# Row stores from ScalarE's queue, a rearranged first group, and a last group in two halves

## The reference

```python
h = conv1d(x, L0_cond_weight, groups=4, taps=9) + ctx + bias    # ctx = cond_128 @ c_weight.T
logits = h @ W_gate + b_gate                                    # 8 experts, the best 2 for each row of 512
y = relu(einsum(h, W_e) + b_e) of the 2 chosen, averaged
x = x + y
m = einsum('boi,bih->boh', agg_w, x) + agg_b[:, :, None]        # 32x32 kernel of each sample, from an MLP on cond_128
W = scales * q - zeros                                          # int4 weights, 512x512
out = x + (m @ W + bias)
```

## Time and profile before

| | us |
|---|---|
| median of 3 runs | 496.83 (495.22 to 497.33) |
| the profiled execution's own time | 496.38 |
| its span, first to last instruction | 494.6 |
| TensorE busy | 480.0 |
| VectorE busy | 322.6 |
| ScalarE busy | 177.1 |
| GpSimd busy | 197.1 |

### The profile page before, as it was taken

The page is one execution under the profiler, slowest core; times in us unless marked ns, Lnnn a source line. Parts: engine busy times, 40 slices in busy tenths (PEclk is TensorE's granted clock), DMA queues, the critical chain, the costliest instruction groups (busy, mean ns, idle before and its releaser), DMA issues.

```text
span 494.6 us, 10082 instructions
## 1 busy us (share of the span) xinstructions
PE 480.0 (97%) x2341; PEld 324.6 (66%) x2342; DVE 322.6 (65%) x966; ACT 177.1 (36%) x309; POOL 197.1 (40%) x215
## 2 busy tenths in 40 slices
PE   7999999999999999999999999999999969999996
PEld 6999999998854444444444444444446748888885
DVE  5688788888748557563453535454356758888885
ACT  5687888889612112121212212112123212211221
POOL 8055555555537533233233332332233334433430
PEclk8899999999999999999999999999999999999999
DMA  6899988997867775787756657565656599999932
GB/s 165 228 324 306 279 279 281 329 303 252 256 160 223 228 218 130 184 233 188 205 151 167 194 143 202 158 184 168 184 154 197 169 346 326 292 326 312 312 121 97
DMA packets 90050, 110.94 MB, mean 224 GB/s; under 512 B 25198, under 2 KB 61726, under 8 KB 88980
## 3 DMA queue, kind: packets, MB, share of 16 engines
q1 hardware_dynamic: 71520, 68.10, 49.3%
q0 software_dynamic: 11952, 37.28, 21.1%
q10 hardware_dynamic: 6536, 5.09, 3.9%
HBM read 65.44 MB, written 46.51 MB: 226 GB/s over the span
## 4 chain that ended last, share of the span: by engine, by line
PE 83%; DVE 6%; DMA 3%; issue 2%; SPq 2%; ACT 1%; ACTq 1%; DVEq 1%; POOL 0%; POOLq 0%
PE bank L1311 40%; PE bank L1285 15%; PE bank L1272 7%; PE bank L1375 5%; PE bank L1371 5%; PE bank L1354 5%; PE bank L1383 2%; PE bank L1361 2%; DMA out<-orow_list 1%; SPq L454 1%; DMA keys<-lists_d 1%; DMA we<-pairs_d 1%; DVE phases L387 1%; DVE ring_a L1004 1%; DVE lT L990 0%
## 5 line engine op out<-in xcount | busy, mean ns | idle before, releaser
L1311 PE MATMUL bank<-we,lT 128*128 x536 | 232.3, 594 | 0.9 <-DVE ring_a L1004 0.8
L1311 PEld LDWEIGHTS bank<-we,lT 128*128 128x128 f32 x536 | 101.1, 190 | 127.5 <-issue 127.3
L575 POOL DMA_INDIRECT pairs_d<-ring_b,pair_i x71 | 71.8, 1012 | 150.5 <-DVE pair_i L993 106.4
L1004 DVE TENSOR_TENSOR ring_a<-bank,be_bc 128x512 f32<-128x512 f32 x71 | 49.1, 691 | 98.4 <-issue 47.3
L671 ACT ACTIVATE ring_b<-ring_a 128x512 f32<-128x512 f32 x71 | 44.7, 630 | 191.5 <-DVE ring_a L1004 176.3
L556 POOL DMA_INDIRECT lists_d<-token_list,row_i x64 | 69.4, 1085 | 71.4 <-issue 33.4
L1285 PE MATMUL bank<-wconv,phases 128*128 128x128 f32 x768 | 93.9, 280 | 0.8 <-ACT phases L387 0.8
L1285 PEld LDWEIGHTS bank<-wconv,phases 128*128 128x128 f32 x768 | 90.8, 196 | 2.5 <-issue 1.5
L387 DVE COPY phases<-xt 32x512 f32<-32x512 f32 (+1 forms) x96 | 52.6, 547 | 9.2 <-PE bank L1285 5.9
L591 POOL TENSOR_TENSOR we<-xt,we 128x512 f32<-128x512 f32 x26 | 33.4, 1284 | 59.7 <-DVE we L1128 54.3
L387 ACT COPY phases<-xt 32x512 f32<-32x512 f32 x64 | 56.6, 884 | 1.5
(11 more groups left out here) (212 smaller groups left out, 378.5 us busy)
## 6 DMA issues: line engine op xcount, KB each, us to landing
xt<-lists_d SPq DMA_DIRECT2D x268, 64.0 KB
xt<-in_x SPq DMA_DIRECT2D x58, 256.0 KB, 4.9
we<-pairs_d SPq DMA_DIRECT2D x26, 512.0 KB, 5.8
we<-in_L_ffn_W_e SPq DMA_DIRECT2D x8, 1024.0 KB
out<-orow_list SPq DMA_DIRECT2D x32, 256.0 KB, 5.1
words<-pairs_d POOLq DMA_DIRECT2D x6, 512.0 KB, 5.1
lists_d<-orow_list SPq DMA_DIRECT2D x8, 257.0 KB
be_bc<-in_L_ffn_b_e ACTq DMA_DIRECT2D x4, 512.0 KB
```

The lines of the kernel that those rows point to most:

```text
L575: pool.indirect_dma_start(pairs_d, bass.IndirectOffsetOnAxis(ap=pair_i[:, s % DR:s % DR + 1], axis=0), ring_b[:, s % U, :], None, bounds_c ...
L1004: dve.tensor_tensor(ring_a[:, j % 2, :], ps_exp[j % 2][:, :], be_bc[:, bass.ds(expert, 1), :].rearrange("p a n -> p (a n)"), ALU.add).then ...
L1311: mm = pe.matmul(ps_exp[j % 2][:, :], lT[:, j, p * P:(p + 1) * P], we[:, bass.ds(expert, 1), p, :].rearrange("m a n -> m (a n)"), start=(p ...
```

## The change

1. SP issues three of the four loads of convolution weights instead of two; ScalarE issues one, and the load of `bg_bc` moves behind its taps.
2. Phases 3 (ScalarE) and 0 and 1 (DVE) of group 0 are copied ahead of the taps. DVE picks 8 of the 12 taps and ScalarE 4. Phase 2 of group 0 is all DVE's, between its taps and the `wconv` copies, so that `step1` of ScalarE skips group 0.
3. TensorE's first warm-up has 20 transposes instead of 24, and two more follow the filter transposes of each shift.
4. All row stores but the last are issued by ScalarE. SP issues the loads of the last phase without stores between them.
5. GpSimd's add of group a waits for the finished `y` of group a-2 (and of the first six) instead of a-1.
6. The last group's linear product is made in two halves of 256 columns, in two PSUM banks; each half is scaled, added and stored by itself. Its terms go to `ps_mix[0]`, are copied by ScalarE to `last_sum` and added to `y` by GpSimd.

```diff
--- before.py
+++ after.py
@@ -248,6 +248,8 @@
         ps_mix, ps_lin, ps_terms, ps_low = bank[4:6], bank[0:4], bank[6:8], bank[0:2]
+        last_bank = [ps_lin[(NG - 1) % U], ps_lin[NG % U]]
+        last_sum = ring_a[:, 0, :]
@@ -369,10 +376,13 @@
+        taps_of_dve = [range(3), range(3), range(2)]
+        taps_of_act = [range(3, PH), range(3, PH), range(2, PH)]
         def pick_taps(copy, phases_of, taps_ready):
             for t in range(SHIFTS):
-                for p in phases_of:
+                for p in phases_of[t]:
                     k0 = PH * t - p + PH - 1
@@ -394,7 +404,7 @@
             sp.wait_ge(wfull_zero, 1)
-            for s in range(2):
+            for s in range(3):
                 rows = slice(s * CG, (s + 1) * CG)
@@ -469,10 +479,6 @@
-            def store_row(g):
-                sp.wait_ge(out_ready, g + 1)
-                sp.dma_start(out_g[g], orow[:, g % 2, :]).then_inc(out_out[g % 2], 16)
             def load_group(a):
@@ -483,24 +489,19 @@
             sp.wait_ge(exp_done, NT)
-            store_row(0)
             for i, done in enumerate(result_out):
...
             load_pairs(PRIMED + 1)
-            store_row(1)
-            for a in range(PRIMED + 2, PRIMED + DEPTH + 2):
+            for a in range(PRIMED + 2, NG):
                 load_group(a)
-            def row_step(g, j):
-                store_row(g)
-                a = g + PRIMED + DEPTH
-                if a < NG:
-                    load_group(a)
-            unrolled(row_step, 2, NG)
-            for s in out_out:
-                sp.wait_ge(s, 16 * (NG // 2))
+            for half in range(2):
+                cols = slice(half * L // 2, (half + 1) * L // 2)
+                sp.wait_ge(half_out, half + 1)
+                sp.dma_start(out_g[NG - 1][:, cols], orow[:, (NG - 1) % 2, cols]).then_inc(out_out[(NG - 1) % 2], 16)
+            for i, s in enumerate(out_out):
+                sp.wait_ge(s, 16 * (NG // 2 + i))
@@ -586,22 +587,26 @@
                 pool.wait_ge(pairs_in[a % FR], (a - PRIMED) // FR * 16 + 16)
-                pool.wait_ge(y_ready, a)
+                pool.wait_ge(y_ready, max(PRIMED, a - 1))
                 wait(pool, out_ready, a - FR + 1)
                 pool.tensor_tensor(y_of(a), xt[:, x_buffer(a), :], found[:, a % FR, 0, :], ALU.add).then_inc(ya_ready, 1)
+            pool.wait_ge(last_read, 1)
+            pool.tensor_tensor(y_of(NG - 1), y_of(NG - 1), last_sum, ALU.add).then_inc(last_y, 1)
...
             act.wait_ge(wfull_zero, 1)
-            for s in range(2, C // CG):
-                rows = slice(s * CG, (s + 1) * CG)
-                act.dma_start(wfull[rows, rows, PH - 1:PH - 1 + TAPS], conv_w[rows]).then_inc(convw_in, 16)
-            act.dma_start(bg_bc[:, :], b_gate.rearrange("(a e) -> a e", a=1).to_broadcast((P, E))).then_inc(bg_in, 16)
+            rows = slice(3 * CG, 4 * CG)
+            act.dma_start(wfull[rows, rows, PH - 1:PH - 1 + TAPS], conv_w[rows]).then_inc(convw_in, 16)
             act.wait_ge(ident_ready, 2)
             act.copy(g0[:, 0:1], ident[:, 0:1])
+            act.wait_ge(pads_ready, 2)
+            act.wait_ge(x_in[0], 16)
+            split_phase(act.copy, 3, 0, 0).then_inc(act_split, 1)
             act.wait_ge(convw_in, 16 * (C // CG))
-            pick_taps(act.copy, range(PH // 2, PH), act_taps)
+            pick_taps(act.copy, taps_of_act, act_taps)
+            act.dma_start(bg_bc[:, :], b_gate.rearrange("(a e) -> a e", a=1).to_broadcast((P, E))).then_inc(bg_in, 16)
@@ -611,7 +616,8 @@
                 a = g + 2
-                if live(a, NG):
+                first = isinstance(g, int) and a == 0
+                if live(a, NG) and not first:
@@ -656,7 +662,6 @@
-            act.wait_ge(pads_ready, 2)
             stepped(act, step1, -2, lo1, hi1, NG + 2)
@@ -723,6 +728,11 @@
+            def store_row(g):
+                act.wait_ge(out_ready, g + 1)
+                act.dma_start(out_g[g], orow[:, g % 2, :]).then_inc(out_out[g % 2], 16)
             stepped(act, step2, 28, 28, hi2, hi2)
@@ -740,9 +750,14 @@
                 high_part(a + 1)
+                store_row(a - 2)
                 if a > 2:
...
                 high_sums(a + 1)
+                store_row(a - 1)
+            act.wait_ge(last_ready, 1)
+            act.copy(last_sum, ps_mix[0][:, :]).then_inc(last_read, 1)
+            store_row(NG - 2)
@@ -760,13 +775,13 @@
+            split_x(0, 0)
             dve.wait_ge(convw_in, 16 * (C // CG))
-            pick_taps(dve.tensor_copy, range(PH // 2), dve_taps)
-            split_x(0, 0)
+            pick_taps(dve.tensor_copy, taps_of_dve, dve_taps)
+            split_phase(dve.tensor_copy, 2, 0, 0).then_inc(dve_split, 1)
             for t in range(SHIFTS):
...
                 dve.tensor_copy(wconv[:, t, :, :].rearrange("k p o -> k (p o)"), ps_w[t][:, 0:P]).then_inc(wconv_ready, 1)
-            split_third(0)
             dve.wait_ge(condT_done, 2)
@@ -1188,9 +1203,25 @@
                 pair_step(a)
-            scale_bank(NG - 1)
+            def scale_half(half):
+                cols = slice(half * L // 2, (half + 1) * L // 2)
+                dve.wait_ge(lin_done, NG + half)
+                dve.tensor_tensor(last_bank[half][:, cols], last_bank[half][:, cols], scale_bc[:, cols], ALU.mult).then_inc(half_scaled, 1)
+            def out_half(half):
+                cols = slice(half * L // 2, (half + 1) * L // 2)
+                dve.wait_ge(half_scaled, half + 1)
+                dve.wait_ge(last_y, 1)
+                dve.wait_ge(out_out[(NG - 1) % 2], 16 * (NG // 2 - 1))
+                dve.tensor_tensor(orow[:, (NG - 1) % 2, cols], last_bank[half][:, cols], y_of(NG - 1)[:, cols], ALU.add).then_inc(half_out, 1)
+            scale_half(0)
             out_row(NG - 2)
-            out_row(NG - 1)
+            out_half(0)
+            scale_half(1)
+            out_half(1)
@@ -1201,7 +1232,7 @@
             pe.wait_ge(ident_ready, 2)
-            warm_up(3 * WARM_START)
+            warm_up(5 * WARM_START // 2)
             for t in range(SHIFTS):
@@ -1209,6 +1240,7 @@
                 mm.then_inc(wT_done, 1)
+                warm_up(2)
             pe.wait_ge(cond_in, 32)
@@ -1376,6 +1408,29 @@
+            def last_terms():
+                pe.wait_ge(tlow_ready, NG)
+                pe.wait_ge(low_ready, NG - 1)
+                pe.matmul(ps_mix[0][:, :], token_rows[:, (NG - 1) * P:NG * P], terms_w[:, :],
+                          start=True, stop=True).then_inc(last_ready, 1)
+            def last_linear():
+                wait(pe, high_ready, NG)
+                wait(pe, low_ready, NG)
+                for half in range(2):
+                    wait(pe, out_ready, NG - U + half)
+                    bank = last_bank[half]
+                    cols = slice(half * L // 2, (half + 1) * L // 2)
+                    for part in (high, low):
+                        for q in range(PH):
+                            mm = pe.matmul(bank[:, cols], part[:, (NG - 1) % 2, q * P:(q + 1) * P], wq[:, q, cols],
+                                           start=(part is high and q == 0), stop=(part is low and q == PH - 1), skip_group_check=True)
+                    mm.then_inc(lin_done, 1)
+                    if half == 0:
+                        add_terms(NG - 2)
             def add_terms(c):
@@ -1392,8 +1447,12 @@
                 linear(a, a % U)
-                linear(a + 1, (a + 1) % U)
-                add_terms(a)
+                if a + 2 < NG:
+                    linear(a + 1, (a + 1) % U)
+                    add_terms(a)
+                else:
+                    last_terms()
+                    last_linear()
@@ -1416,7 +1475,6 @@
                 pair_step(a)
-            add_terms(NG - 1)
```

More of the change, by code:

```diff
@@ L335, in build_program @@
         scaled_ready = sem("scaled_ready")
+        last_ready = sem("last_ready")
+        last_read = sem("last_read")
+        last_y = sem("last_y")
+        half_scaled = sem("half_scaled")
+        half_out = sem("half_out")
         out_ready = sem("out_ready")
```

## The result

The changed kernel took 498.58 us in the median of 11 runs (496.05 to 500.45), the kernel before 495.81 us in 11 runs of the same comparison (493.09 to 499.96). The ratio is 1.006, with a 95% interval of 1.0037 to 1.0082: slower, by a little more than half a per cent. 489.2 us was forecast, and 498.58 lies above the range (486.5 to 493.5). The profiled execution took 498.24 us.

What follows compares the result with a forecast made beforehand. PE was taken as the bound, busy 97% of the span; gains of 1.9 (head), 4.9 (seam) and 0.5 (tail), 7.3 us off 496.38, gave 489.1, stated as 489.2 us against the runs' median; range 486.5 to 493.5.

Steps and rivals of the forecast that it cites:

- the seam: Start of the last phase: earlier row stores and GpSimd's relaxed wait shorten a stretch from 11.61 to 6.74, gaining 4.9 us.
- the tail: After the last linear product: halved scaling, add and store end sooner, gaining 0.5 us (0 to 0.9).
- late stores: Rival at the start of the last phase: stores take 7.3 us, seam gains 1.3, total 3.7: 492.7 us; chance 0.15.
- The tail's step: Kernel end: the last terms pass through ScalarE (0.59) and GpSimd (1.27) beside PE, to about 490.5 us.
- The seam's step: Start of the last phase: row 2's store, issued near 393.4, takes 4.3 us to land, between bounds 2.0 and 7.3.
- The step on GpSimd: Start of the last phase: the relaxed wait lets group 7's add run near 393.7 instead of 397.64; finish_y(7) follows at once.
- a store has no load ahead in its own queue: Last phase: argument against the slower rival, in which stores at 7.3 us throughout give 511 us; chance 0.05.
- The head's start: First group: convolution 0 starts at 8.6 us instead of 9.51, gaining 0.9 us, or 0.5 if something is late.
- clock never falls: Rival in the first group: PE keeps full clock, convolution 0 takes 2.8 us, 1.7 more gained: 487.5 us; chance 0.3.
- PE has no long idle behind it, so the gain reaches the end: After the first group: the head's whole gain of 1.9 us (0.5 to 3.6) carries through to the kernel's end.
- loads held to 293 GB/s: Last phase: at this DMA rate the loads end at 479.4 and 2.1 us of the 4.9 come back.
- store latency as the period: Slower rival in the last phase: pairs exceed 6.74 us from 6.0 us of sustained store latency; 511 us at 7.3; chance 0.05.

Runs made afterwards that it cites:

- tail_dve: The changed kernel, but VectorE adds the last group's terms to y straight from PSUM, without ScalarE's copy and GpSimd's add: 492.12 us, ratio 0.9946 to the kernel before.

## Why the prediction was wrong

Two steps failed. The profiled span was to fall by 7.3 us and rose by 1.9; against the forecast the seam is 6.2 us worse and the tail 3.35, and the rest 0.35 better. The seam is the larger miss, but the tail's is what made the change slower: with the drain out of the way it takes 492.12 us, inside the range and near the rival "late stores" (492.7).

**The tail's step: "The terms pass through ScalarE (0.59) and GpSimd (1.27) beside PE, to about 490.5."** The passing is beside PE, as said, though with nothing to spare: GpSimd's add ended at 489.38, and DVE's first half add began at 489.46. What I left out is that GpSimd's last instruction carries a closing drain of 6.9 to 7.0 us behind it. The drain was in the trace of before, ending at 486.8, and none of the prediction's rows has it. From DVE's last add to the end of the span it is 5.8 us in after and 2.2 with the add on DVE: 3.6 us. The tail was put down as 0.5 us of gain, and it lost 2.85 (0.41 won, 3.26 lost). The rest of the tail was a little better than costed: each half of the product took 1.0 us as said (487.21 to 488.17, where the terms' matmul starts), and the last add came 0.41 us sooner after the last mixes, where about 0.25 was forecast. Without the drain the halves are worth 0.9 us by the profiles, the top of the range of 0 to 0.9.

**The seam's step: "I take 4.3, the shortest of the three in the seam."** The store of row 1 took 7.74 us and that of row 2 8.1. The forecast priced only row 2's, though the change took something from row 1's: in the kernel before SP issued it at 391.82, ahead of `load_group(8)` (392.20), and it landed after 3.7 us. With the stores gone from its queue, SP issued the loads of groups 8 and 9 first, by 389.5. The rival "late stores" had the mechanism and the latency (7.3), at a chance of 0.15, and the place too, the pair that row 1's store holds up. It was dearer than it said: PE's idle time let the clock go to 0.50 for 6.8 us (397.6 to 404.4), which cost 3.73 less 1.95 for the mixes alone; the second stretch took 9.09 us where the rival had 6.74. So the seam gave −1.3 where the rival said +1.3 and the forecast 4.9.

That is one execution, and the seam varies. With the stores on ScalarE's queue and the loads free it took 20.3, 19.1, 17.5 and 17.5 us in four profiles; with the old order 18.9, 19.7, 19.7 and 18.4. The means, 18.6 and 19.2, differ by 0.6 us the other way, less than either scatters: the −1.3 is in part chance, and the 4.9 is in none of the four. Running the stores alone confirms that little or nothing is in it (1.0015), and the held-back loads with landings of 4.0 us show that the forecast's latency hung on what SP had issued before. The step on GpSimd held: it added groups 6 and 7 one after the other from 390.50 on, and `finish_y(7)` followed `finish_y(6)` at once.

Another sentence fell, "a store has no load ahead in its own queue": true of the queue, and of no use. Lines of the queues in after, in four stretches of one microsecond, from 391, 393, 394 and 396 (packets, MB, share of the 16 engines):

```profile
q1 hardware_dynamic: 156, 0.33, 100.1%
...
q1 hardware_dynamic: 124, 0.29, 94.8%
q10 hardware_dynamic: 5, 0.01, 2.6%
...
q1 hardware_dynamic: 111, 0.29, 81.4%
q10 hardware_dynamic: 47, 0.10, 24.6%
...
q1 hardware_dynamic: 100, 0.20, 52.5%
q10 hardware_dynamic: 102, 0.19, 49.8%
```

q1 is SP's queue, q10 ScalarE's. Row 1's store was issued at 389.57, and its queue moved no packet until 393.8. SP's moved 1.4 MB in that time; 2.6 MB of loads had been issued there from 386.56 to 389.5. From 394 to 395 SP's moved three times as much as ScalarE's, and from 396 to 397 the two shared about evenly. The Trainium skill's sentence that I had weighed against the change (DMA: Bandwidth & Descriptors, section Issuing engines are not separate DMA queues) has the outcome right: a second issuer bought an earlier issue and no more, here as in the stores alone. Its section on queues, rings and completion order, with engines that alternate between queues by packets, describes the time from 396, not that from 389.57 to 393.8.

**The head's start held, and its clock was the better case.** Start 8.68 (forecast 8.6; in six kernels with the new head 8.54 to 10.20, in seven with an old one 9.33 to 9.51); duration 2.95, which is the rival "clock never falls" (2.8; chance 0.3) and not the forecast's 4.4. Whether the change did that is not shown: convolution 0 took 2.92 to 2.95 us in four kernels with the new head and 4.57 and 4.93 in two, and with an old head 5.48 or 5.49 in five, 4.57 in one and 2.94 in one (the stores alone). **"PE has no long idle behind it, so the gain reaches the end"** failed: of 3.54 us at the gate of group 0, 1.5 went at groups 5 and 6, where x is late for a DVE that now comes sooner. That 1.94 us of the lead was left at the seam, where 1.9 was forecast, is luck: a larger gain, less a loss that wasn't forecast. By profiles, the first linear product starts at 376.5 us in the mean of six kernels with the new head (374.77 to 377.56) and at 378.4 in seven with an old one (377.10 to 379.00), 1.9 us. With the same new head the gate of group 0 started between 15.12 and 18.77, with an old one between 16.09 and 18.80. The times give 0.13% with an interval of 0.34% either way for the head alone, and 0.0006 between the two four-buffer kernels that differ in it. Its worth, between nothing and some 2 us, **stays open**.

The sum, as the profiles have it, against the forecast's 1.9 + 4.9 + 0.5: 1.94 − 1.31 + 0.32 (steady pairs, not forecast) + 0.41 − 3.26 = −1.9 us of span. Two sums of the prediction are slightly off, and neither matters here: loads held to 293 GB/s would end 2.4 us late and not 2.1, and 7.3 us off the runs' median of 496.83 is 489.5 and not 489.2.

**The chances.** 0.06 for slower was too small, and its one mechanism (store latency as the period) isn't what happened: pairs behind the seam ran at 6.71 us. The slower case came from GpSimd's closing drain, which no rival of the prediction has.

## What to carry to other kernels

Before work is moved to the end of a kernel on an engine that had finished, look up what that engine does after its last instruction, and when, in the closing lines of the trace; for GpSimd here, an instruction that ends less than some 7 us before the last store lands should lengthen the kernel (one ending at 489.38 and one at 491.2 did, one ending at 480.6 didn't; nothing between was tried). When an engine waits for a store before it may reuse a buffer, and moving the store's issue only moves the wait to the next row, count the buffers against latency: two more of them brought what three reorderings couldn't. A latency taken from a trace belongs to the backlog it was measured behind; ask what will be in front of the transfer after the change.

## What the runs showed that was unexpected

- GpSimd's closing drain: 6972 and 6973 ns behind a memset of 0.10 us, 8182 to 8207 ns counted from about the start of an add of 1.3 us in the eleven other profiles. It doesn't depend on how long before the kernel's end it starts (465.5 to 491.1).
- A store issued by ScalarE behind 2.6 MB of SP's loads moved no packet for 4.2 us, though it is in another queue, and landed after 7.7 to 8.1 us; with SP's last loads held back it landed after 4.0. That something ahead of the two queues is shared would fit this; no run shows it.
- PE's granted clock fell to 0.50 in after when PE had stood still from 394.88 to 397.6, and came back at 404.4. It stayed at 1.00 through 402 to 406 in before, where PE was busy 1.10 of 4.00 us with 2.90 us of it in one wait, and at 1.00 through a wait of 2.78 us in `tail_dve`.
